# A Mamba audio tower: B broadcast by TensorE transposes of a repeated column, five of eight state pairs turned, one of them a POOL product

## The reference, cut to what matters

```python
xc = silu(conv(xi) + conv_b)                      # xi, z: halves of x @ in_proj
dt, Bm, Cm = split(xc @ x_proj, [8, 24])          # 8 + 16 + 16 columns
delta = softplus(dt @ dt_w + dt_b)                # 256 channels
def step(h, inp):                                 # 250 steps, h is 256 x 16
    xt, dt_, bt, ct = inp
    dA = exp(dt_[..., None] * A)
    h = dA * h + dt_[..., None] * bt[:, None, :] * xt[..., None]
    y = einsum('bdn,bn->bd', h, ct)
    return (h, y)
y = (ys + xc * Dv) * silu(z)
out = y @ out_proj
```

## Time and profile before

| | |
|---|---|
| median of 3 runs | 3480.59 us (3477.56 to 3481.06) |
| profiled execution | 3478.78 us, its span 3477.0 us |
| busy DVE / ACT | 3042.4 us (88%) / 3106.2 us (89%) |
| busy PE / POOL | 2952.8 us (85%) / 2824.1 us (81%) |
| mean granted TensorE clock | 0.981 |
| chain that ended last | ACT 33%, PE 31%, DVE 20%, issue 14% |

### The profile page before, as it was taken

The page is one execution under the profiler, slowest core; times in us unless marked ns, Lnnn a source line. Parts: engine busy times, 40 slices in busy tenths (PEclk is TensorE's granted clock), DMA queues, the critical chain, the costliest instruction groups (busy, mean ns, idle before and its releaser), DMA issues.

```text
span 3477.0 us, 53162 instructions
## 1 busy us (share of the span) xinstructions
PE 2952.8 (85%) x18432; PEld 2224.8 (64%) x18432; DVE 3042.4 (88%) x2456; ACT 3106.2 (89%) x5825; POOL 2824.1 (81%) x1701
## 2 busy tenths in 40 slices
PE   5888888888888888888888888888888888888885
PEld 3666666666666666666666666666666666666664
DVE  3889889889889888898898898899898988888986
ACT  4989999999989999999999998999999999999984
POOL 2788888888888888788788888888887888888886
PEclk9999999999999999999999999999999999999998
DMA  2222222222222222222222222222222222222221
GB/s 72 89 72 92 86 86 85 81 83 91 86 86 85 78 91 86 81 88 83 82 86 86 86 91 73 91 85 86 87 89 74 91 86 85 85 81 83 87 81 48
DMA packets 102319, 290.59 MB, mean 84 GB/s; under 512 B 11387, under 2 KB 36262, under 8 KB 102054
## 3 DMA queue, kind: packets, MB, share of 16 engines
q1 hardware_dynamic: 102054, 287.19, 25.4%
HBM read 276.91 MB, written 10.24 MB: 83 GB/s over the span
## 4 chain that ended last, share of the span: by engine, by line
ACT 33%; PE 31%; DVE 20%; issue 14%; POOL 1%; DVEq 0%; SPq 0%; DMA 0%; ACTq 0%; POOLq 0%
ACT da L697 13%; DVE hc L941 10%; PE g_ps L329 8%; DVE g_ps L928 8%; ACT w L643 7%; PE y_ps L329 5%; ACT L684 5%; PE m_ps L362 3%; PE m_ps L413 3%; PE m_ps L371 3%; PE m_ps L329 3%; PE m_ps L429 2%; PE m_ps L391 2%; DVE stats L914 2%; ACT s L667 1%
## 5 line engine op out<-in xcount | busy, mean ns | idle before, releaser
L834 POOL TENSOR_TENSOR hc<-hc,c_all 128x1000 f32<-128x1000 f32 x1024 | 2350.3, 2313 | 522.3 <-DVE hc L941 508.4
L941 DVE TENSOR_TENSOR_SCAN hc<-da,g_ps 128x1012 f32<-128x1012 f32 x1024 | 2274.6, 2253 | 91.4 <-ACT da L697 18.9
L697 ACT ACTIVATE da<-delta,a_neg 128x498 f32<-128x498 f32 x2048 | 1332.9, 700 | 9.0 <-DVE hc L941 7.3
L329 PEld LDWEIGHTS y_ps<-ident,hc 128*125 128x125 f32 x8192 | 1027.7, 190 | 238.8 <-issue 164.3
L329 PE MATMUL y_ps<-ident,hc 128*125 128x128 f32 x8192 | 1081.7, 275 | 2.2 <-POOL hc L834 2.2
L643 ACT ACTIVATE w<-ut,bt 125x256 f32<-125x256 f32 x2048 | 892.8, 497 | 2.9 <-ACT ut L630 0.4
L329 PE MATMUL g_ps<-ident,w 125*128 125x125 f32 x4096 | 547.3, 277 | 370.7 <-DVE hc L941 280.5
L329 PEld LDWEIGHTS g_ps<-ident,w 125*128 125x128 f32 x4096 | 443.9, 142 | 427.1 <-DVE hc L941 326.1
L928 DVE TENSOR_TENSOR g_ps<-u,g_ps 128x1000 f32<-128x1000 f32 x512 | 608.2, 1188 | 80.6 <-PE g_ps L455 80.3
L362 PE MATMUL m_ps<-zt,convw 128*128 128x500 f32 x1024 | 475.6, 587 | 0.7 <-ACT zt L573 0.7
L362 PEld LDWEIGHTS m_ps<-zt,convw 128*128 128x128 f32 x1024 | 190.5, 191 | 148.7 <-issue 121.9
(11 more groups left out here) (62 smaller groups left out, 2314.5 us busy)
## 6 DMA issues: line engine op xcount, KB each, us to landing
c_all<-c_rows SPq DMA_DIRECT2D x512, 500.0 KB, 3.6
xin<-x_t SPq DMA_DIRECT2D x32, 375.0 KB, 3.5
out<-out_sb SPq DMA_DIRECT2D x32, 250.0 KB
c_rows<-dbl SPq DMA_DIRECT2D x64, 31.2 KB, 1.6
c_all<-f_conv_w SPq DMA_DIRECT2D x1, 512.0 KB
c_all<-b_conv_w SPq DMA_DIRECT2D x1, 512.0 KB
hc<-f_in_w SPq DMA_DIRECT2D x1, 128.0 KB
inw<-f_in_w SPq DMA_DIRECT2D x1, 128.0 KB
```

What stands on the lines that cost most here:

```text
L329: return pe.matmul(dst, src, ident[0:rows, 0:rows], start=first, stop=last, is_transpose=True, skip_group_check=True)
L697: op = act.activation(states(da[n % RING])[j].rearrange("p (s t) -> p s t", s=SC)[:, :, 1:T], steps, ACT.Exp, scale=a_neg[:, p % 2, db, 2 ...
L834: pool.tensor_tensor(hc, hc, c_all[:, pair % CRING], ALU.mult).then_inc(hc_ready, 1)
L941: dve.tensor_tensor_scan(h[n % HRING][:, 0:UC], da[n % RING][:], g_ps[n % 2][:, 0:UC], 0.0, ALU.mult, ALU.add).then_inc(scanned, 1)
```

## The change

- Five pairs are turned: 2, 5, 6 and 7 by ACT as before, at other steps, and pair 3 by POOL, as two products of tensors of 125 x 1024 (`make_w`, all four token groups of a state at once, with the column of B repeated 256 times by a stride of 0), at steps 0 and 2.
- Pairs 0, 1 and 4 get B by transposes: the stationary operand is one column of bt repeated 128 times, the moving one the identity. `fill_g` is then 8 transposes for every unit.
- The three bf16 parts, both splits, the selecting matrices and their two loads are gone.
- DVE's product `times_b` is made for 6 units of a phase, where there were 8.
- The jobs stand at other steps: `dt_proj` 7 (softplus on ACT 8), `turn_b` 8, `y_back` 9 and 10, `turn_u` 12 and 13, `turn` and the first half of `out_proj` 13.

The core of the diff:

```diff
-CONV, GATES, XPROJ, BT, SPLIT1, Y0, SPLIT2, Y1, DT, U0, U1, UT0, UT1 = 0, 4, 5, 6, 6, 6, 7, 8, 9, 11, 12, 13, 14
-TURN, TAIL0, TAIL1, TOKENS = 10, 11, 14, 15
+CONV, GATES, XPROJ, DT, SOFTPLUS, BT, Y0, Y1, U0, U1, UT0, UT1 = 0, 4, 5, 7, 8, 8, 9, 10, 10, 11, 12, 13
+TURN, TAIL0, TAIL1, TOKENS = 13, 13, 14, 15
-W_ACT = {2: [(-2, 4), (-1, 4)], 4: [(0, 2), (1, 2), (2, 2), (3, 2)], 6: [(6, 3), (7, 3), (8, 2)], 7: [(10, 2), (11, 3), (12, 3)]}
-W_POOL = {}
+W_ACT = {2: [(-2, 4), (-1, 4)], 5: [(0, 2), (1, 2), (2, 2), (3, 2)], 6: [(5, 3), (6, 3), (7, 2)], 7: [(9, 2), (10, 2), (11, 2), (12, 2)]}
+W_POOL = {3: [(0, 1), (2, 1)]}
...
-                    src = w[w_index(p, r) % WRING]
-                    for e in range(2):
-                        for j in range(NT):
-                            at = e * BANK + j * TP
-                            mm = turned(g[:, at:at + TP], src[:, e, j, db * 128:(db + 1) * 128], TP)
-                    mm.then_inc(b_filled, 1)
-                else:
-                    if k <= 1:
-                        wait_drained(pe, "split", p, 2)
-                    pe.matmul(g[:, 0:TC], pick[:, 2 * r, :], parts[p % 2][:], start=True, stop=True)
-                    pe.matmul(g[:, BANK:UC], pick[:, 2 * r + 1, :], parts[p % 2][:],
-                              start=True, stop=True).then_inc(b_filled, 1)
+                elif k <= 1:
+                    wait_drained(pe, "bt", p, 0)
+                for e in range(2):
+                    for j in range(NT):
+                        if r in TURNED:
+                            rows = w[w_index(p, r) % WRING][:, e, j, db * 128:(db + 1) * 128]
+                        else:
+                            rows = bt[p % 2][:, j, 2 * r + e:2 * r + e + 1].broadcast_to([TP, 128])
+                        at = e * BANK + j * TP
+                        mm = turned(g[:, at:at + TP], rows, TP)
+                mm.then_inc(b_filled, 1)
...
-                op = pool.tensor_scalar(w[w_index(p, r) % WRING][:, e, j, :], ut[p % 2][:, j, :],
-                                        bt[p % 2][:, j, 2 * r + e:2 * r + e + 1], None, ALU.mult)
-                if n == 2 * NT - 1:
+                b_cols = bt[p % 2][:, :, 2 * r + n:2 * r + n + 1].broadcast_to([TP, NT, DI])
+                op = pool.tensor_tensor(w[w_index(p, r) % WRING][:, n], ut[p % 2][:], b_cols, ALU.mult)
+                if n == 1:
...
-                    if m > 0 and k in (Y0 + 1, Y1 + 1):
-                        gated(m - 1, 0 if k == Y0 + 1 else 1)
+                    if m > 0 and k in (Y0 + 2, Y1 + 2):
+                        gated(m - 1, 0 if k == Y0 + 2 else 1)
```

More of the change, by code:

```diff
@@ L96, in front_jobs @@
 def front_jobs(m):
[L100 to L103, removed]
+    ends = [("y", m - 2, 0), ("y", m - 2, 1)] if m > 1 else []
+    return ([("conv", m, 0), ("conv", m, 1), ("gate", m, 0), ("gate", m, 1), ("xproj", m, 0),
+             ("dt", m, 0), ("dt", m, 1), ("bt", m, 0)] + ends, [("ut", m, 0), ("ut", m, 1)])
 def all_jobs():
@@ L380, in xproj @@
                 mm.then_inc(job_filled, 1)
[L382 to L386, removed]
             def dt_proj(p, db):
@@ L479, in _ @@
             xproj(0)
+            dt_proj(0, 0)
+            dt_proj(0, 1)
             turn_b(0)
[L481 to L484, removed]
             turn_u(0, 0)
@@ L504, in _ @@
                             xproj(m + 1)
+                        if k == DT:
+                            dt_proj(m + 1, 0)
+                            dt_proj(m + 1, 1)
                         if k == BT:
                             turn_b(m + 1)
-                        if k == SPLIT1:
-                            split(m + 1, 1)
                     if m > 0 and k == Y0:
                         y_back(m - 1, 0)
-                    if m == 0 and k == Y0:
-                        dt_proj(1, 0)
-                    if front and k == SPLIT2:
-                        split(m + 1, 2)
                     if m > 0 and k == Y1:
                         y_back(m - 1, 1)
-                    if front and k == DT:
-                        if m > 0:
-                            dt_proj(m + 1, 0)
-                        dt_proj(m + 1, 1)
-                    if more and k == TURN:
-                        turn(i + 1)
-                    if d == 0 and i > 0 and k == TAIL0:
-                        out_proj(i - 1, 0)
                     if front:
@@ L529, in _ @@
                             turn_u(m + 1, 1)
+                    if more and k == TURN:
+                        turn(i + 1)
+                    if d == 0 and i > 0 and k == TAIL0:
+                        out_proj(i - 1, 0)
                     if d == 0 and i > 0 and k == TAIL1:
@@ L598, in xproj @@
                     act.wait_ge(c_written, 16 * p)
-                if p > 1:
-                    act.wait_ge(b_filled, UNITS * (p - 1))
                 m = bank("xproj", p, 0)
-                act.activation(dbl[:], m[0:XR, 0:TC], ACT.Copy)
-                act.activation(parts[p % 2][:], m[0:K2, 0:TC],
-                               ACT.Copy).then_inc(drained[bank_of("xproj", p, 0)], 1)
-            def split(p, n):
-                m = bank("split", p, n)
-                act.activation(parts[p % 2][:], m[0:K2, 0:TC], ACT.Copy).then_inc(drained[bank_of("split", p, n)], 1)
+                act.activation(dbl[:], m[0:XR, 0:TC], ACT.Copy).then_inc(drained[bank_of("xproj", p, 0)], 1)
             def softplus(p, db):
@@ L751, in _ @@
                             load_set(EXP_SET)
+                        if k == BT:
+                            bt_copy(m + 1)
                     if more and k == NORM_Z:
                         norm_z(i + 1)
-                    if more and k == TURN:
-                        zt_copy(i + 1)
-                    if d == 0 and i > 0 and k == TAIL0:
-                        out_half(i - 1, 0)
                     if front:
@@ L762, in _ @@
                             ut_copy(m + 1, 1)
+                    if more and k == TURN:
+                        zt_copy(i + 1)
+                    if d == 0 and i > 0 and k == TAIL0:
+                        out_half(i - 1, 0)
                     if d == 0 and i > 0 and k == TAIL1:
```

37 lines of the change are left out of this document (10 added, 27 removed).

## The result

The changed kernel takes **3556.04 us** (median, 3555.39 to 3557.68) where the kernel before takes 3479.07 on the same chip: a ratio of **1.0223**, with a 95% interval of 1.0207 to 1.0239. It is slower by 77 us. I had forecast slower by 0.5% (3498); the sign held, the size was off by 58 us.

What follows compares the result with a forecast made beforehand. Bound: a cycle of PE's steps, ACT's steps 4 to 8, then PE again, with DVE beside it. Chunk 104.28 + 2.05 = 106.33 against 105.65, + 22 over 32 chunks, less 4.5 at the start: 3498 us, range 3415 to 3575.

Steps and rivals of the forecast that it cites:

- Schedule without the clock: Step-by-step count of PE's and ACT's work over both phases: 54.32 + 49.96 = 104.28 us a chunk, against 105.04 undisturbed before.
- `turn_b`'s waits: PE standing before step 8's transposes for the bank softplus frees: 3.96 us with d = 1, 2.55 with d = 0.
- DVE's 5.24 us: DVE's two products fewer per phase, 5.24 us a chunk; only 0.76 of it was to be left in the chunk.
- The clock term: Half-clock dips after PE's idle at turn_b: 0.95 x 1.5 (d = 1) and 0.5 x 1.3 (d = 0), 2.05 a chunk, before 0.61.
- The start: Before the first product: loads and casts gone and two splits fewer in the first front, about 4.5 us less.
- POOL's products: Four products of 125 x 1024 a chunk on POOL, 2.33 us each, 9.3 us a chunk, hidden with about 1 us to spare.
- The upper bound of double: Stride-0 operand makes POOL's products cost up to twice, 4.7 us each; rival: chunk 108.5, about 3570 us, chance 0.07.
- The clock holds: Rival: no dip on PE beyond today's, chunk 104.28 + 0.61 = 104.89, about 3452 us; chance 0.22.
- More hand-overs bind: Rival: more hand-overs between engines bind than counted, each 1 to 2 us a chunk, 3520 to 3560 us; chance 0.16.
- DVE's saving comes through: Rival: ACT or PE has unseen slack, so up to 168 us is saved, 3308 to 3440, middle 3410; chance 0.08.
- Transposes alone let the clock fall: Rival: PE's steps 11 to 15 take 3.56 instead of 1.78, 10 to 12 us a chunk, about 3840; chance 0.04.
- The signs: Profile after: turn_b waiting 2 to 4 us, PE clock below 0.981, DVE near 2885 busy, POOL products 2.35, first product 58.

## Why the prediction was wrong in size

- **Schedule without the clock, 104.28 us: right.** The chunk with the filled gap is 104.20 in the middle of the run and 103.86 on the mean; both phases agree within 0.25; `turn_b`'s waits were 3.96 and 2.55 by hand and 3.92 and 2.38 in the trace. That only a little of DVE's 5.24 us would be left was right too: leaving the fifth pair out changed the chunk by 0.09.
- **The clock term, 2.05 us a chunk: this is the step that failed.** Its mechanism is right, PE stands and 1.2 GHz follows, but the term measures 4.36. I priced the two dips one by one and added them: 0.95 x 1.5 and 0.5 x 1.3 (which make 2.08, not 2.05). Each price was close: a dip alone costs 1.59 in either phase. Two things were missing. The dip of the d = 0 phase, taken as even, came at nearly every wait; two certain dips of 1.59 make 3.18. And two dips in one chunk cost 1.18 more than twice one. In the chunk shown the d = 1 phase takes 57.75 us, against 54.46 with the gaps filled, and the d = 0 phase 51.40 against 49.74. A longer wait is not the reason, since the same 3.93 us with the other gap filled has the short dip; why two dips cost more than their sum stays open. The term is short by 2.31 a chunk, 74 us; the schedule's mean, better than forecast by 0.42, gives 13 back. Of before's 105.65 the clock held 0.69, not 0.61, which changes nothing in the sum.
- **So of the change's +2.57 a chunk,** 4.36 - 0.69 = +3.67 is clock and 103.86 - 104.96 = -1.10 is a shorter schedule. Without the clock the change would be a gain of 35 us at the chunks; with both gaps filled, the two kernels stand at 3418.5 and 3455.5.
- **The start, 4.5 us less: right** (62.32 to 56.98, 5.3).
- **POOL's products: too dear.** 1.907 us instead of 2.33; four a chunk are 1.7 us less on an engine that was off the path by my count, and no run tells what they moved. The upper bound of double did not come. The rival built on it falls.
- **"The clock holds", 3452:** not what happened. Filling the gap made the case, with no dip in the middle of the run, and gave 3418.5. The number was too high by the 0.61 of dips that it kept and by the 0.42 of the schedule.
- **"More hand-overs bind", 3520 to 3560,** holds the measured time, but not its reason: the hand-overs bound as counted.
- **"DVE's saving comes through"** is false in this order, and in the order of before with the transposes half of it comes through.
- **"Transposes alone let the clock fall":** false. Kernels made of as many transposes ran at 0.994 and 0.995, and 15 us of nothing but transposes at 1.00. The Trainium skill's sentence that the full rate doesn't engage for them ("TensorE: Matmul & The Clock Gate", PE-mode transpose) does not agree with these runs.
- **The signs:** `turn_b`'s wait, the mean clock (0.953), DVE's busy time (2913 us for 2885), its idle time (207 us more for 190) and the first product (57 us for 58) came as said; the 2.35 us of POOL's products did not.
- **Slips that move nothing:** 45.11 - 41.17 is 3.94, not 3.96; POOL's work per chunk is 88.3 us, not 89 (the 107.0 goes by 88.3); with half of 0.43 the chances of slower add to 0.49, not 0.53. The function set is loaded four times per phase, not three: 64 and 191 loads over the run.

## What to carry to other kernels

A wait of PE of some microseconds is to be priced twice: as itself, where it is on the path, and as the transposes and matmuls behind it at half clock, which the trace shows with their durations doubled; ask of each moved step how long PE will stand with nothing to do, and don't add up dips that were priced one by one. A wait that is taken away can come back behind the same engine a few steps on: of the 2.0 us saved at `turn_b` with d = 0, 1.9 stood at a later fill. A cheap test is to put matmuls that add zero into the gap: if the time falls, the clock was the cost, and then the order of hand-overs is worth changing. And work taken off an engine shows only in an order where that engine's waits don't end on the others: the same pair was worth nothing (1 us), 17 us of loss and 84 us of gain in three orders of nearly the same work (in the second the clock also fell more often).

## What was new about the hardware here

- Useless matmuls made the kernel faster: PE's mean granted clock rose from 0.953 to 0.994 and 137.5 us went. In the kernel before, two such matmuls a chunk brought 23 us.
- A wait of the same length is followed by a fall or not: that of 1.90 us in 16 of 30 chunks before, that of 2.74 us in 22 of 31 with `turn_b` at step 6, and that of 2.38 us in 32 of 33 in the changed kernel. In the two kernels with transposes in the old order no wait of up to 1.75 us has one between 200 and 3300 us.
- The same idle time of 3.92 and 3.93 us at the same place was followed by about 7 us at 1.2 GHz in one kernel and by about 3.5 in another, and one dip or two a chunk cost 1.6 and 4.36 us. Two kernels with quite different waits (the changed one, and before with late gated products) have periods near each other, 109.15 and 109.1 to 109.4, and the two with one gap filled share 105.8 to 105.9. What sets these steps stays open.
- On POOL a product of 125 x 1024 with one operand repeated by a stride of 0 takes 1.907 us on the mean of 128, where 128 x 1000 with two full operands takes 2.314 on the mean of 1024.
- Eight transposes whose stationary operand is one column repeated 128 times cost what eight with a full tile cost (0.86 from start to start for both).
